# First-chunk preparation moved into the convolution, shared buffers, and the skip sum cut into regions

## The reference, cut to what matters

```python
xz = x @ W_in.T;  xc, z = split(xz)               # 256 channels each
xc = silu(conv3x3_depthwise(xc) + conv_b)
x1 = local_scan(xc)                               # 16x16 windows, row order
x2 = local_scan(xc, column_first=True)            # 16x16 windows, column order
xs = [x1, x2, flip(x1), flip(x2)]                 # 4 directions, 4096 tokens each
dts, Bs, Cs = split(xs @ x_proj)                  # 8 + 16 + 16 rows per direction
delta = softplus(dts @ dt_proj + dt_bias)
h = exp(delta * A) * h + (delta * u) * B          # 16 states per channel, token by token
y = sum(h * C) + u * D                            # u * D is the skipped input
y = y0 + inv(y2) + turned(y1) + turned(inv(y3))
out = (layernorm(y) * silu(z)) @ W_out.T
```

## Time and profile before

| What | Value |
|---|---|
| Median of three runs | 6255.01 us |
| Profiled execution, its own time | 6258.71 us |
| Span of the profiled execution | 6256.9 us |
| Granted TensorE clock, mean | 0.969 |
| PE, VectorE, ScalarE, GpSimd busy | 91%, 71%, 51%, 45% |

### The profile page before, as it was taken

How to read it: one execution, slowest core, us unless ns; L and a number is a source line. 1 busy time by engine, 2 the same in 40 slices (tenths; PEclk the granted TensorE clock), 3 DMA queues, 4 the chain that set the end, 5 groups by cost and what they waited for, 6 DMA issues and landing times. The chain is left out here.

```text
span 6256.9 us, 128558 instructions
## 1 busy us (share of the span) xinstructions
PE 5702.8 (91%) x41691; PEld 5079.1 (81%) x41691; DVE 4472.1 (71%) x6306; ACT 3169.5 (51%) x6029; POOL 2832.3 (45%) x1695
## 2 busy tenths in 40 slices
PE   7899999999888999999997659999999899999998
PEld 5688888888667888888885538888888788888887
DVE  2699999999618999999995645555555555555554
ACT  2699888988638998899885221111111111111110
POOL 1699999999608999999994300000000000000000
PEclk8899999999989999999999879999999999999999
DMA  2455555555415555555554147776766666777765
GB/s 96 113 141 144 139 142 143 142 143 137 121 56 136 143 143 139 138 145 145 141 138 124 43 128 156 149 152 147 153 151 149 164 140 151 148 154 149 149 150 143
DMA packets 1098945, 858.32 MB, mean 137 GB/s; under 512 B 305622, under 2 KB 1021238, under 8 KB 1064374
## 3 DMA queue, kind: packets, MB, share of 16 engines
q1 hardware_dynamic: 1097974, 844.72, 55.8%
q10 hardware_dynamic: 720, 10.49, 0.4%
HBM read 811.50 MB, written 43.55 MB: 137 GB/s over the span
## 5 line engine op out<-in xcount | busy, mean ns | idle before, releaser
L726 POOL TENSOR_TENSOR read<-state,c_wide 128x1024 f32<-128x1024 f32 x1024 | 2419.3, 2379 | 213.5 <-DVE state L762 127.3
L762 DVE TENSOR_TENSOR_SCAN state<-decay,carry,p_drive 128x512 f32<-128x512 f32 x1792 | 2140.5, 1258 | 104.0 <-PE p_drive L540 57.2
L658 ACT ACTIVATE decay<-step,a_neg 128x512 f32<-128x512 f32 x2048 | 1398.1, 717 | 223.8 <-DVE state L762 214.3
L1747 PE MATMUL p_y<-window,x_high 128*128 128x256 f32 x7936 | 1495.9, 286 | 0.0
L1811 ACT COPY term_blocks<-p_s 128x256 f32<-128x256 f32 x832 | 310.5, 373 | 2157.2 <-PE p_s L1747 2157.2
L1747 PEld LDWEIGHTS p_y<-window,x_high 128*128 128x128 f32 x7936 | 1243.6, 191 | 0.0
L1747 PE MATMUL p_y<-window,x_low 128*128 128x256 f32 x3968 | 1132.5, 285 | 0.0
L553 PE MATMUL p_y<-ident,read 128*128 128x128 f32 x8192 | 1064.1, 273 | 13.0 <-ACT y_tok L672 3.7
L542 PE MATMUL p_drive<-diag_b,xu_tok 128*128 128x128 f32 x8192 | 1002.7, 276 | 1.3 <-DVE state L762 1.3
L542 PEld LDWEIGHTS p_drive<-diag_b,xu_tok 128*128 128x128 f32 x8192 | 959.2, 193 | 1.6 <-DVE state L762 1.6
L553 PEld LDWEIGHTS p_y<-ident,read 128*128 128x128 f32 x8192 | 925.2, 141 | 25.5 <-issue 21.7
(11 more groups left out here) (257 smaller groups left out, 5443.7 us busy)
## 6 DMA issues: line engine op xcount, KB each, us to landing
c_wide<-c_scratch SPq DMA_DIRECT2D x256, 1024.0 KB, 4.8
window<-taps_scratch SPq DMA_DIRECT2D x576, 257.0 KB, 6.4
diag_b<-diag_scratch SPq DMA_DIRECT2D x256, 512.0 KB, 4.1
window<-taps_scratch SPq DMA_DIRECT2D x768, 129.0 KB, 5.1
window<-taps_scratch SPq DMA_DIRECT2D x128, 513.0 KB, 7.3
window<-taps_scratch SPq DMA_DIRECT2D x64, 385.0 KB, 6.2
gate_scratch<-gate_out SPq DMA_DIRECT2D x16, 512.0 KB, 3.1
gate_in<-gate_scratch SPq DMA_DIRECT2D x8, 1024.0 KB, 6.3
```

The lines of the kernel that those rows point to most:

```text
L658: act.activation(decay[:, n % 2, t, :], step[:, c.parity, t, :], ACT.Exp, scale=m.a_neg[:, DT2 * c.k + t, n:n + 1]).then_inc(s["decay"], 1)
L726: pool.tensor_tensor(read[:, n % 4, :, :], state[:, n % 4, :, :], wide, ALU.mult).then_inc(s["read_out"], 1)
L762: dve.tensor_tensor_scan(flip(state[:, n % 4, t, :], c), flip(decay[:, n % 2, t, :], c), flip(p_drive[:, n % 2, t, :], c), 0.0 if c.start ...
L1747: last = pe.matmul(out, x[:, source, blk, :], view[:, :, at:at + P][:, :, ::-1], start=first and x is m.x_high and z == 0, stop=True, skip ...
```

## The change

The preparation's functions move into a class that both blocks use. The convolution now calls them for chunk 0 between its units; its loops over g are unrolled. `begin_y` is replaced by `add_second`, which sums the second part of the skipped input by regions of the image: three of the four groups in the convolution, the last at the head of the scans. The order at the head of `scans` is then `times_b(0)`, the first decays, `times_b(2)` on ScalarE, `drive(0)`, `drive(1)` on PE, two `add_second` on VectorE, and the loads of SP. x_tok, the gate buffers and the scans' xd, step, softplus, xu_tok and b_tok share one allocation, and the PSUM tiles p_prep and p_b serve both blocks.

```diff
 def convolution(nc, m, io, b):
-        x_tok = sb("x_tok", [P, T // P, C])
+        x_tok = m.x_tok
+        prep, chunk = Preparation(m), Chunk(b, 0, 0, 0, 0, first=True)
-        gate = sb("gate_out", [P, 2, DT2, L])
+        gate = m.gate
-        pt = [ctx.enter_context(nc.psum_tensor(f"pt{i}", [P, L], fp32)) for i in range(2)]
+        pt = [m.p_prep, m.p_b]
...
# SP
-            with sp.Fori(0, NG) as g:
+            for g in range(NG):
...
+                if g == 1:
+                    prep.store_rows(sp, nc, chunk)
# GpSimd
-            with pool.Fori(0, NG) as g:
+            for g in range(NG):
...
+                                       ALU.mult).then_inc(m.sem_b["y_begun"], 1)
+                if g == 1:
+                    prep.step_times_u(pool, chunk)
# PE, after the 30 matmuls of a unit
-            with pe.Fori(0, NG) as g:
+            for g in range(NG):
...
+                        unit = 4 * g + 2 * half + t
+                        if unit == 5:
+                            pe.wait_ge(s["gated"], START + b * 17 + 5)
+                            prep.project(pe, chunk)
+                        if unit == 6:
+                            prep.step_product(pe, chunk, 0)
+                            prep.step_product(pe, chunk, 1)
+                        if unit == 7:
+                            prep.turn_b(pe, chunk)
+                        if unit in (11, 12):
+                            prep.turn_x(pe, chunk, unit - 11)
# ScalarE, after the three silu of a unit
-            with act.Fori(0, NG) as g:
+            for g in range(NG):
...
+                        if unit == 5:
+                            prep.keep_projection(act, chunk)
+                        if unit == 6:
+                            prep.step_parts(act, chunk)
+                        if unit == 7:
+                            prep.keep_b(act, chunk)
+                            act.preload_act_table_set("natural_log_exp_and_others")
+                            prep.step_exp(act, chunk)
+                            prep.step_ln(act, chunk)
+                        if unit in (11, 12):
+                            prep.keep_x(act, chunk, unit - 11)
# VectorE, after the norm
+            for g in range(NG - 1):
+                for t in range(DT2):
+                    dve.wait_ge(s["gated"], START + b * 17 + g * 4 + (4 + t))
+                    dve.wait_ge(m.sem_b["y_begun"], START + b * 8 + (2 * g + t + 1))
+                    add_second(dve, m, g, t)
+                if g == 1:
+                    prep.finish_step(dve, chunk)
...
+def add_second(dve, m, g, t):
+    y = m.y[:, t, :].rearrange("p (h w) -> p w h", w=W)
+    x = m.s2[:, t, :].rearrange("p (w h) -> p w h", h=H)
+    new, past = slice(WIN * g, WIN * (g + 1)), slice(0, WIN * g)
+    last = g == NCH // 2 - 1
+    pieces = [(slice(0, W), new)] if last else []
+    for w in range(0, W, WIN):
+        pieces.append((slice(w + 4 * g, w + 4 * g + 4), past if last else slice(0, WIN * (g + 1))))
+        if g and not last:
+            pieces.append((slice(w, w + 4 * g), new))
+    for columns, rows in pieces:
+        ins = dve.scalar_tensor_tensor(y[:, columns, rows], x[:, columns, rows], m.d_skip[:, 10 + t:11 + t],
+                                       y[:, columns, rows], ALU.mult, ALU.add)
+    return ins
...
 def scans(nc, m, b):        # the heads of the five bodies
-                    store_rows(c)                                  # SP
                     sp.wait_ge(s["c_stored"], START + c.g * 32 + 32)
-                    project(c)                                     # PE
...
-                    keep_projection(c)                             # ScalarE
...
-                if c.first:
-                    step_times_u(c)                                # GpSimd
-                    begin_y(0)                                     # VectorE
-                    finish_step(c)
-                    begin_y(1)
+                    for t in range(DT2):
+                        add_second(dve, m, 3, t).then_inc(s["y_whole"], 1)
...
+            ready = sb0("chunk_ready", [P, XD + 2 * NB4 * NS + 10 * L])
+            m.x_tok = ready[:, 0:T // P * C].rearrange("p (t c) -> p t c", c=C)
...
+            m.gate = [m.step[:, 1], m.xu_tok[:, 1].rearrange("p (t i) d -> p t (i d)", t=DT2)]
```

More of the change, by code:

```diff
@@ L26 @@
 ODD = NS // 2
+XD = L
 START = 16
@@ L318, in _ @@
                         act.wait_ge(s["gate_out"][half], START + b * 64 + g * 16)
-                        act.activation(gate[:, half, t, :], pz[t][:, :], ACT.Silu).then_inc(s["gated"], 1)
+                        act.activation(gate[half][:, t, :], pz[t][:, :], ACT.Silu).then_inc(s["gated"], 1)
+                        unit = 4 * g + 2 * half + t
+                        if unit == 5:
[9 more added lines that the diff above has]
+                            prep.keep_x(act, chunk, unit - 11)
         @block.vector
@@ L439, in _ @@
         def _(sp):
[L440 to L449, removed]
             def load_diag(c, d):
@@ L491, in _ @@
         def _(pe):
[L492 to L527, removed]
             def drive(c, n):
@@ L659, in decays @@
                                scale=m.a_neg[:, DT2 * c.k + t, n:n + 1]).then_inc(s["decay"], 1)
-            def keep_x(c, half):
-                act.wait_ge(s["x_turned"], START + c.g * 2 + (half + 1))
-                if not c.first:
-                    act.wait_ge(s["scaled"], START + c.g * ODD + -ODD)
-                    act.wait_ge(s["driven"], START + c.q * 2 + -2 * NS)
-                act.copy(xu_tok[:, c.parity, 2 * half:2 * half + 2, :],
-                         p_prep[:, :].rearrange("p (i d) -> p i d", d=DI)).then_inc(s["x_kept"], 1)
             def keep_y(c):
@@ L743, in _ @@
         def _(dve):
-            def begin_y(t):
-                y = m.y[:, t, :].rearrange("p (h w) -> p w h", w=W)
-                dve.scalar_tensor_tensor(y, m.s2[:, t, :].rearrange("p (w h) -> p w h", h=H), m.d_skip[:, 10 + t:11 + t], y,
-                                         ALU.mult, ALU.add).then_inc(s["y_begun"], 1)
-            def finish_step(c):
-                dve.wait_ge(s["step_ln"], START + c.g + 1)
-                dve.tensor_tensor(step[:, c.parity, :, :], step[:, c.parity, :, :], softplus,
-                                  ALU.add).then_inc(s["step"], 1)
             def scan(c, n, t):
@@ L780, in body @@
                 if c.first:
-                    begin_y(0)
-                    finish_step(c)
-                    begin_y(1)
+                    for t in range(DT2):
+                        add_second(dve, m, 3, t).then_inc(s["y_whole"], 1)
                 for n in range(NS):
```

207 lines of the change are left out of this document (133 added, 74 removed).

## The result

The changed kernel took 6238.8 us (median of 8 runs, 6232.2 to 6243.9), the kernel before 6258.8 us (8 runs). The ratio is 0.9968 with an interval of 0.9959 to 0.9977: 20 us faster (14 to 26), half of the forecast 39.8 us. 6215.2 us and the range up to 6229 us were both missed.

A forecast was written before the change was run, and what follows sets the result against it. PE bounds the convolution; mid-scan all four engines are busy 91 to 96%, so only edges count. 2 x (23.6 - 5.2) + 3 = 39.8 us off the 6255.0 us median gave 6215.2 us, range 6203 to 6229 us.

The forecast's parts named there:

- Head, 8.7 us: Head of the scans: VectorE's two add_second delay the first scan by 8.7 us instead of 32.3, gaining 23.6 an image.
- Convolution, 5.2 us: PE's added projection, step products and transposes lengthen the PE-bound convolution by 5.2 us an image, bounds 4.7 to 7.
- rival A: Convolution: step*u arrives after unit 11 and PE stands waiting; 6235 to 6255 us, chance 0.04.
- B: Rival: the last region's sums cost more, 12.5 us at the head and 7 us on PE; 6229 us, chance 0.11.
- C: Rival: the convolution's unrolled matmuls run faster, 960 of them winning 0.010 us each; 6206 us, chance 0.08.
- D: Rival: unrolled code feeds PE too slowly at L285, slower from 0.280 us a matmul, 6274 us at 0.30; chance 0.03.
- this is at full clock, which the convolution has: Starting point for PE's additions in the convolution, 5.2 us an image: PE's granted clock is 1.00 there.
- The fill, 3 us: First states of the scans: GpSimd's fifth read starts earlier, winning 3 us over both images, bounds 0 and 7.
- And so warm up: First states: while VectorE delays the first scan 4.6 us, PE makes drive(0), drive(1) and the next projection, warming up.
- 13.2 us for the fifth read: First states: GpSimd's fifth read starts 13.2 us after the first scan, 1.3 and 3.4 us earlier than before.
- A difference of two stages, it carries over as it is: Whole kernel: the 39.8 us gain summed from the profile applies unchanged to the median, giving 6215.2 us.

The follow-up runs named there:

- the control: The changed kernel with 128 memsets added on VectorE at the program's start: 6241.0 us, ratio 0.9966 to the kernel before.
- the shift back: The changed kernel with 68 single-column memsets added on VectorE at the program's start: 6232.1 us, ratio 0.9951 to the kernel before.
- the shift of the kernel before: The kernel before with 60 single-column memsets added on VectorE at the program's start: 6276.9 us, ratio 1.0025 to the kernel before.
- With fetches and fill mended: The changed kernel with 68 memsets on VectorE at the start and 24 PE transposes in the first chunk: 6221.2 us, ratio 0.9934 to the kernel before.

## Why the prediction was wrong

*Head, 8.7 us*: right, 8.4; VectorE's own sums were late next, and ten pieces over the rate of a whole sum cost 8.46 - 7.8 us, some 0.06 us each where I had 0.08. *Convolution, 5.2 us*: right for the profiled execution, 4.9, but in part by luck. PE's project took 1.88 us, the two step products 2.1, the first transposes 0.60. Nobody waited for the preparation (rival A): step*u began at 130.1 us, took 2.40, and PE asked for it 19 us after its end. B, C and D didn't come about either. But "this is at full clock, which the convolution has" is not safe: in half of the convolutions profiled the clock falls behind the step products, which costs some 2 us an image (9 of 18 convolutions; the rows stand above).

*The fill, 3 us*: a step of it failed. "And so warm up" took for granted that a PE that is warm once stays so. It then idled for 1.7 us, fell back to 1.2 GHz, and the first sum_y came late. The estimate of 13.2 us for the fifth read was right for a warm PE. With the control beside it, the missing warmth is worth 8.2 us over both images (two medians of five runs, each spreading by 12 to 15 us), and chunks 0 and 1 of the same two profiles give 7.9 us; beside the profiled changed kernel, which had a milder fall in image 0, they give 5.1 us.

*"A difference of two stages, it carries over as it is"*: the step that failed. 39.8 us were worked out from the order and the durations of instructions. That the program's other code moves when instructions are added ahead of it, and that a loop can pay for its place, was no term of the sum and no rival, although the profile's page lists the fetches. By the shift back it is worth 8.9 us (68 against 128), by the shift of the kernel before 15.9 (10 to 21), by the chunks 10.9.

In the profiled pair the forecast is missed by 14.6 us: 10.9 by the repeated fetches, 3.9 by the fill, 4.1 after the last sum, less 4.3 in the rest. The medians miss it by 20 us, since a usual execution of the changed kernel is 5.3 us longer than the profiled one. The control shows where such a one can lose it: it had the fall of the clock in the convolution of image 0 and the longer fall at the fill in both images.

With fetches and fill mended the median gain is 41 us, close to the forecast's 39.8, but that is in part luck. The profile of that kernel is 36.2 us shorter than the one before: 47.9 at the heads, less 14.6 in the convolutions where the forecast had 10.4, plus 5.7 in the scans where it had 3, less 2.7 after the last sum. That last stage stays open. Its first part, to the first matmul of the spectral stage, took 408.1 us in the one profile before, 411.2 us in the shifted kernel before and 410.1 to 414.2 in the others.

The range failed for the same reason as the number: each of its bounds was the bound of a term that I had named.

## What to carry to other kernels

When a change adds or removes instructions ahead of a runtime loop, compare the instruction rows of the DMA queues and the length of each turn far behind the change; a stop at every turn that names a different releaser each time, and new fetches beside it, is the loop's place in the program. A few dozen idle instructions in a stretch where the engine waits anyway test it, but their number counts: 24 and 68 healed this kernel, 44 moved the loss to another loop, 128 changed nothing. And a gain at the edge of a pipeline is whole only if the engine that fills it is kept busy through the filling. Look at the granted clock behind every piece of light work that a change puts into a busy stream, too.

## What the runs showed of the hardware that I had not expected

- Instructions of VectorE come in pieces of 8192 bytes. By the count of instructions, a loop of 280 over three pieces ran through its turns without a fetch; over four, it took five fetches a turn of 89 us, stood 1.4 to 2.3 us at the turn, and cost 1 to 7 us an image and direction (9 to 16 us by medians for two directions in two images).
- The releaser that the trace names for such a stop was not its cause: it named drives and decays of other engines, and 68 memsets on VectorE alone took the waits away.
- PE fell to the 1.2 GHz level after an idle time of only 1.7 us with light work around it; 24 small transposes prevented that in all four images of the two kernels that had them and were otherwise in the same order; with VectorE's sums behind the eighth scan it fell again, 8 us later. In the convolution it fell without such an idle time, behind the step products, in 9 of 18 cases.
- Strided sums on VectorE and GpSimd's products hold each other up: whole sums of 8.9 us stop GpSimd altogether (10.93 instead of 2.37 us), short pieces share the loss (6.32 instead of 4.23, and 4.11 instead of 2.37).
